# A causal mask for row maxima, moved from TensorE's identity matmuls to VectorE's fused add-and-max

## The reference

```python
qkv = jnp.einsum('bnd,ed->bne', inputs, w_in)
scores = jnp.einsum('bhqd,bhkd->bhqk', q, k) * Hd ** (-0.5)
causal = jnp.triu(jnp.ones((N, N), dtype=bool), k=1)
scores = jnp.where(causal, -jnp.inf, scores)
attn = jax.nn.softmax(scores, axis=-1)
out = jnp.einsum('bhqk,bhkd->bhqd', attn, v)
...
x = x + ga * _L0_attn_ref(h, ...)
h = _layernorm(x, axis=-1) * (1 + cb) + sb
x = x + gb * _L0_ffn_ref(h, ...)      # r * (square(relu(xk @ W_k.T)) @ W_v.T), r = sigmoid(xr @ W_r.T)
```

## Time and profile before

| | |
|---|---|
| Time, median of 3 runs | 1754.11 us (1753.4 to 1755.41) |
| Span of the profiled execution | 1747.5 us |
| The profiled execution's own time | not recorded apart from its span; the median lies 6.6 us above the span |
| Busy, share of the span | PE 84%, PEld 44%, DVE 67%, ACT 52%, POOL 42% |
| Instructions | PE 10024, DVE 2307, ACT 1795, POOL 876 |
| Mean granted TensorE clock | 0.930 |
| Chain that ended last, by engine | PE 49%, DVE 21%, issue 12%, ACT 9%, POOL 6% |

### The profile page before, as it was taken

How to read it: one execution, slowest core, us unless ns; L and a number is a source line. 1 busy time by engine, 2 the same in 40 slices (tenths; PEclk the granted TensorE clock), 3 DMA queues, 4 the chain that set the end, 5 groups by cost and what they waited for, 6 DMA issues and landing times.

```text
span 1747.5 us, 33032 instructions
## 1 busy us (share of the span) xinstructions
PE 1460.0 (84%) x10024; PEld 767.3 (44%) x10024; DVE 1176.4 (67%) x2307; ACT 911.6 (52%) x1795; POOL 731.7 (42%) x876
## 2 busy tenths in 40 slices
PE   2599999889897888879888898978889799889754
PEld 2343435444543445444444445434454344544344
DVE  4368677867677775767767775787757777677232
ACT  1146555555565554555555554555545655555622
POOL 2213213445344443544334553344434443444555
PEclk8679999899998999999998999989999999999966
DMA  3111113111311113111221113111131111211200
GB/s 103 38 64 57 45 57 100 44 50 55 99 56 35 56 57 97 57 42 51 74 79 41 54 56 95 58 39 54 53 94 66 39 51 65 67 56 44 60 28 18
DMA packets 101873, 102.98 MB, mean 59 GB/s; under 512 B 21296, under 2 KB 89912, under 8 KB 101696
## 3 DMA queue, kind: packets, MB, share of 16 engines
q1 hardware_dynamic: 99136, 92.38, 16.3%
q0 software_dynamic: 2560, 8.39, 1.3%
HBM read 31.74 MB, written 8.94 MB: 23 GB/s over the span
## 4 chain that ended last, share of the span: by engine, by line
PE 49%; DVE 21%; issue 12%; ACT 9%; POOL 6%; SPq 2%; DMA 1%; DVEq 1%; ACTq 0%; POOLq 0%
PE row_ps L1058 9%; PE val_ps L1082 9%; PE col_ps L1028 7%; PE dense_ps L1092 7%; DVE max_a L855 6%; PE dense_ps L1093 5%; PE dense_ps L1094 5%; ACT weights L699 4%; DVE mixed L968 2%; DVE max_b L855 2%; PE row_ps L1063 2%; PE dense_ps L1111 2%; SPq L457 2%; DVE xn_c L894 1%; DVE gated L952 1%
## 5 line engine op out<-in xcount | busy, mean ns | idle before, releaser
L699 ACT ACTIVATE weights<-col_ps 128x512 f32<-128x512 f32 (+1 forms) x1216 | 621.0, 580 | 475.3 <-PE col_ps L1028 473.4
L855 DVE TENSOR_REDUCE max_a<-row_ps 128x1 f32<-128x512 f32 (+3 forms) x864 | 550.1, 663 | 249.1 <-PE row_ps L1063 162.1
L1058 PE MATMUL row_ps<-k_stack,q_stack 96*128 96x512 bf16 (+3 forms) x1536 | 470.8, 345 | 52.6 <-DVE max_a L855 32.4
L1028 PE MATMUL col_ps<-q_stack,k_stack 99*128 99x512 bf16 (+3 forms) x1536 | 400.2, 337 | 52.2 <-ACT weights L699 32.3
L590 POOL TENSOR_SCALAR_AFFINE_SELECT weights<-weights 128x512 f32<-128x512 f32 x256 | 170.1, 664 | 557.9 <-ACT weights L699 555.9
L1082 PE MATMUL val_ps<-weights,v_ones 128*32 128x512 f32 (+3 forms) x3072 | 336.5, 511 | 15.5 <-POOL weights L590 15.2
L1058 PEld LDWEIGHTS row_ps<-k_stack,q_stack 96*128 96x128 bf16 x1536 | 147.4, 100 | 353.9 <-DVE max_a L855 166.8
L855 DVE TENSOR_REDUCE max_b<-row_ps 128x1 f32<-128x384 f32 (+3 forms) x352 | 213.2, 635 | 120.4 <-PE row_ps L1063 120.1
L1028 PEld LDWEIGHTS col_ps<-q_stack,k_stack 99*128 99x128 bf16 x1536 | 133.9, 99 | 219.8 <-ACT weights L699 136.8
L1063 PE MATMUL row_ps<-causal,ident_bf 128*128 128x128 bf16 x1024 | 208.5, 228 | 0.0
L1063 PEld LDWEIGHTS row_ps<-causal,ident_bf 128*128 128x128 bf16 x1024 | 104.9, 102 | 15.0 <-issue 0.7
(11 more groups left out here) (128 smaller groups left out, 2290.0 us busy)
## 6 DMA issues: line engine op xcount, KB each, us to landing
q_stack<-q_part SPq DMA_DIRECT2D x384, 64.0 KB, 2.6
k_stack<-k_part SPq DMA_DIRECT2D x384, 64.0 KB, 2.6
xa<-in_x SPq DMA_DIRECT2D x8, 1024.0 KB, 6.4
att<-val_out SPq DMA_DIRECT2D x64, 128.0 KB
recips<-recip_rows SPq DMA_DIRECT2D x32, 256.0 KB
xq<-in_x SPq DMA_DIRECT2D x28, 256.0 KB, 3.2
out<-xq POOLq DMA_DIRECT2D x28, 256.0 KB, 2.6
q_stack<-max_rows SPq DMA_DIRECT2D x192, 4.0 KB
```

The lines of the kernel that those rows point to most:

```text
L699: nc.scalar.activation(weights[:, t % 2, h:h + n, 0:q1 - q0], col_ps[bank][:, 0:n * (q1 - q0)].rearrange("p (h q) -> p h q", h=n), ACT.Exp ...
L855: nc.vector.reduce_max(dest, bank[:, 0:len(heads) * (k1 - k0)].rearrange("p (h k) -> p h k", h=len(heads)), AX_X).then_inc(max_done, 1)
L1028: last = nc.tensor.matmul(col_ps[bank][:, i * (q1 - q0):(i + 1) * (q1 - q0)], k_stack[s % 2][:, h, P * j:P * (j + 1)], q_stack[s % 2][:, h ...
L1058: last = nc.tensor.matmul(bank[:, n * width:(n + 1) * width], q_stack[stack][0:ROWS, h, P * i:P * (i + 1)], k_stack[stack][0:ROWS, h, k0:k ...
```

## The change

TensorE's masking matmuls are gone. `causal` becomes 512 wide, zeros and then the triangle in its last 128 columns. On VectorE each head of a diagonal unit gets one fused instruction that reads the scores from PSUM and the last `width` columns of `causal` from SBUF, adds them, writes the sum back over the scores in PSUM, and takes the maximum of the sum along the row. Plain units keep their maximum. The wait of every maximum is now one by `wait_apart`. To make room in SBUF, `recept` is dropped: ScalarE writes its tanh into `mix_out` itself, so it waits for `out_done` of the quarter before (VectorE waited for that until now).

```diff
-        causal = sb("causal", [P, P], BF16)
+        causal = sb("causal", [P, HALF], BF16)
...
-        recept = sb("recept", [P, 2, D])
...
                 if u == 10:
                     act.wait_ge(ready["recept"], q + 1)
-                    wait(act, free["value"], q)
-                    nc.scalar.activation(recept[:], dense_ps[:], ACT.Tanh, scale=0.5).then_inc(free["recept"], 1)
+                    wait(act, out_done, q)
+                    nc.scalar.activation(mix_out[:], dense_ps[:], ACT.Tanh, scale=0.5).then_inc(free["recept"], 1)
...
-                dve.wait_ge(rows_ready, at + 1)
+                wait_apart(dve, "dve", rows_ready, at + 1)
...
-                dest = (max_b[:, i - 4] if second else max_a[:, i])[:, heads[0]:heads[-1] + 1]
-                nc.vector.reduce_max(dest, bank[:, 0:len(heads) * (k1 - k0)].rearrange(
-                    "p (h k) -> p h k", h=len(heads)), AX_X).then_inc(max_done, 1)
+                dest, width = max_b[:, i - 4] if second else max_a[:, i], k1 - k0
+                if k1 == P * (i + 1):
+                    for n, h in enumerate(heads):
+                        scores = bank[:, n * width:(n + 1) * width]
+                        last = nc.vector.tensor_tensor_reduce(scores, scores, causal[:, HALF - width:], 1.0, MASKED,
+                                                              ALU.add, ALU.max, dest[:, h:h + 1])
+                    last.then_inc(max_done, 1)
+                else:
+                    nc.vector.reduce_max(dest[:, heads[0]:heads[-1] + 1],
+                                         bank[:, 0:len(heads) * width].rearrange("p (h k) -> p h k", h=len(heads)),
+                                         AX_X).then_inc(max_done, 1)
...
                 if u == 14:
                     dve.wait_ge(ready["value"], q + 1)
-                    wait(dve, out_done, q)
-                    nc.vector.scalar_tensor_tensor(mix_out[:], recept[:], 1.0, dense_ps[:], ALU.add, ALU.mult
+                    nc.vector.scalar_tensor_tensor(mix_out[:], mix_out[:], 1.0, dense_ps[:], ALU.add, ALU.mult
...
-                                            start=(n == 0), stop=(end and not diagonal), skip_group_check=True)
-                    if diagonal:
-                        last = nc.tensor.matmul(bank[:, (n + 1) * width - P:(n + 1) * width], ident_bf[:],
-                                                causal[:], start=False, stop=end, skip_group_check=True)
+                                            start=(n == 0), stop=(n == len(heads) - 1), skip_group_check=True)
```

More of the change, by code:

```diff
@@ L569, in _ @@
                                         pattern=[[-1, P]], channel_multiplier=1)
-            nc.gpsimd.affine_select(out=causal[:], in_=causal[:], compare_op=ALU.is_ge, fill=MASKED, base=0,
-                                    pattern=[[-1, P]], channel_multiplier=1).then_inc(consts_done, 1)
+            nc.gpsimd.affine_select(out=causal[:, HALF - P:], in_=causal[:, HALF - P:], compare_op=ALU.is_ge,
+                                    fill=MASKED, base=0, pattern=[[-1, P]], channel_multiplier=1
+                                    ).then_inc(consts_done, 1)
             pool.wait_ge(consts_done, 1)
@@ L1054, in row_unit @@
                 stack = (s + 1) % 2
-                diagonal = k1 == P * (i + 1)
                 for n, h in enumerate(heads):
-                    end = n == len(heads) - 1
                     last = nc.tensor.matmul(bank[:, n * width:(n + 1) * width],
```

## The result

The changed kernel takes 1822.05 us (1820.87 to 1827.36, 4 runs) against 1753.76: 1.040 times as long, interval 1.0376 to 1.0423, 68 us slower. The forecast was 16. The direction holds; the time lies outside the forecast's own range (1758 to 1800) and, by 3 us, inside the outer one, which ran to 1825. That outer part was put in for another rival, the held read, so that it held the result is luck.

A forecast was written before the change was run, and what follows sets the result against it. It took the kernel as coupled, TensorE with 49% of the chain and VectorE 21%. VectorE +44, TensorE -30 and tanh +2 gave +16 on 1747.5, with the median's 6.6 us 1770 us; own range 1758 to 1800, outer 1736 to 1825.

The forecast's parts named there:

- the held read: Rival on VectorE: the result's read waits until the fused instruction is through; +93 us, 1847 us, chance 0.12.
- how much of it lands on the end: Step taking 24% of VectorE's added 184 us as reaching the span's end: 44 us (26 low, 108 high).
- TensorE's saving: 1024 masking matmuls go from TensorE: 30 us gained, bounds 17 to 61.
- VectorE's prices: VectorE's added work: elements 18 us, reads 123, separate waits 43; 184 us in all (143 low, 348 high).
- The read: VectorE's read of each fused result: 0.12 us, bounds 0.08 to 0.28; 123 us for 1024 reads.
- The separate waits: VectorE's wait as its own instruction: 0.12 us more at 358 starts where it stands waiting, 43 us.
- The tanh: ScalarE's tanh into `mix_out` waits for the add, uncovered only in the drain: 2 us, bounds 0 to 8.
- The extra work hides: Rival: VectorE's added work falls into its idling for TensorE and the masks come off; about -25, 1729 us, chance 0.26.
- no change: Rival: the low ends of the terms meet; -2 us, 1752 us, chance 0.11.
- Half rate of the write back: Rival: VectorE's PSUM write takes turns with its read; 343 us more VectorE work, above 1900 us, chance 0.04.
- The clock: Rival: TensorE, with less work, sits at 1.2 GHz for 4% more of the span; +33 together, 1787 us, chance 0.04.
- What would show it: Signs: VectorE busy 1310 us, pair 0.72 before the next, TensorE's maxima waits above 203, VectorE's row waits below 363.

The follow-up runs named there:

- hold: GpSimd's last step of each group waits until VectorE has cut the second half's maxima; added to the kernel before: 1746.6 us, 0.9976.
- masks_off: The kernel before without TensorE's 1024 masking matmuls, row maxima taken over unmasked scores: 1720.7 us, 0.9857.
- before_late_hold: The kernel before with one short VectorE instruction ahead of the second cut of the maxima, and GpSimd's last step waiting for that cut: 1747.0 us, 1.0007.
- masks_off_fill: The kernel before without masking matmuls, plus 704 extra VectorE maxima over 40 columns, 75 us in all: 1755.6 us, 1.0025.
- after_hold_single: The changed kernel with GpSimd's last step waiting for the cut, fused instruction only in one-head units, others plain maxima over unmasked scores: 1761.7 us, 1.0063.
- before_late: The kernel before with one short VectorE instruction more ahead of the second cut of the maxima, 32 in all: 1790.1 us, 1.0258.
- after_hold: The changed kernel with GpSimd's last step of each group waiting until VectorE has cut the maxima: 1781.5 us, 1.0174.
- masks_off_hold: The kernel before without masking matmuls, maxima over unmasked scores, and GpSimd's last step waiting for VectorE's cut: 1739.1 us, 0.9935.

## Why the prediction was wrong

**The sum, as the runs divide it.** With the collision held off, the parts can be had one after the other: hold in the kernel before -4, masks off -7 (0.9976 to 0.9935), fused instructions with their waits on diagonal units +17 (to 1.0033), tanh into `mix_out` +7 (to 1.0075), separate waits on the other units +17 (to 1.0174), and the collision let in again +40 (to 1.040). Each step is uncertain by 5 to 11 us, so of the small ones -4 is not clear of nothing and -7 and +7 hardly are; 40 is. Together +70, and without the collision +30, which lies inside the forecast's 4 to 45 slower. The order matters: without the hold, masks_off gains 25 us, because it also pulls the cut clear of the select.

**The step that failed** is "how much of it lands on the end". It took what VectorE does more, 184 us, times a share of 24%. That step knows only two outcomes for added work, hidden or passed on. The trace of before held a third: a short instruction that waits behind GpSimd's, with the next, longer GpSimd instruction right after. There 0.2 us of lateness makes the cut 1 us longer in 15 groups more, and this overlap, which before_late_hold takes away, is worth 43 us. This term, 40 us of the 52 by which I was short, is not in the sum. The forecast named what was queued behind a late maximum (layer norm, `gated`, `mixed`), but not the cut, and it never set VectorE's short instructions beside GpSimd's timeline. The sign was there to read: in the earlier trace rows the steps of the cut of the first half take 0.17 us, while in the same trace the last step of the second half took 0.64.

**TensorE's saving,** -30: measured -25 by itself, 27 and 37 when matmuls were added, and 7 with the hold. The size was right for the kernel as it stood.

**VectorE's prices.** Elements 18 us: borne out (a fused instruction costs as much by width as a maximum). The read: taken 0.12, bounds 0.08 to 0.28, measured 0.05 to 0.06 where it is longest and 0.04 on average; 1024 of them are 38 to 61 us instead of 123. So VectorE got at most 73 us of elements and reads, not 141 (8 x (0.65 + 0.52 + 0.38 + 0.25) = 14.4 us a group against 12.1, 32 groups), and by the average 56. The error was in the fast direction and hid part of the other.

**The separate waits:** in the forecast 43 x 0.24 = 10; alone in the kernel before 12, with 4 more collided cuts in it. In the changed kernel with the hold those on plain units and transposes alone are worth 17, uncertain by 11.

**The share.** 17 us of 73, 23%, for the fused part (30% of 56; the waits ahead of it are in the 17); 39% for masks_off_fill, which has some collision in it; 41% for after_hold_single, which has none. These are uncertain by 9, 15 and 23 points. The 24% is at the low end, and the runs don't settle a better number.

**The tanh,** 2 (0 to 8): measured 9 and 7, each uncertain by 4 to 8. I looked for uncovered handovers in the drain alone. Where the rest arises I did not trace.

**The rivals.** *The extra work hides* and *no change* fall: the ratio's interval begins at 1.0376. *The read is held* falls by the timeline: it starts 0.65 us after the start of a fused instruction that lasts 0.73, and the next instruction starts with it. The time itself, 1822, lies where this rival's part of the range was; that is no support for it. The section "The DRAIN you can't avoid" of the Trainium skill's page "VectorE: DVE Perf Modes", which I quoted for it, goes on to say that a next instruction that is not held starts earlier, and the trace agrees with that. *Half rate of the write back* falls: 711 ns, not 1340. *The clock:* it did fall, 0.930 to 0.898 in the profiled executions, but less work on TensorE doesn't lower it (masks_off), and refilling TensorE doesn't help. Part of the fall goes with the collision: the executions of before_late have 0.908 to 0.928, those of before_late_hold 0.929 to 0.948. The collision isn't the only thing that lowers it: after_hold, without it, still has 0.911 to 0.918, and masks_off_hold 0.916 to 0.936.

So part of the 43 and 40 us probably reaches the end by way of the clock. In the profiled executions TensorE is busy for 36 us longer in before_late than in before_late_hold, and for 20 us longer in the changed kernel (1458.4) than in after_hold (1438.5), with the same instructions. Its waits for the cut are longer by 20 and 31 us. If half of the longer rows lands, as TensorE holds 49% of the chain, that makes 38 and 41 us. This is an estimate; no run holds the clock still, and how the loss divides stays open.

**What would show it.** Busy VectorE 1310 or more: 1269. The pair 0.72 before the next: 0.65. TensorE's waits for maxima rose from 203 to 267 us (138.2 + 67.5 + 61.7 in its weight loads) and VectorE's for rows fell from 363 to 348, as expected. Of the groups shown, s=1 kept its length, and s=2 and s=3 grew, where I had expected s=1 to grow and s=3 hardly.

Here are the two lists that hold these sums. Weight loads:

```profile
PEld row_ps L1065 <- DVE max_a L864: 138.2, 190, 2.5
...
PEld row_ps L1065 <- DVE max_a L860: 67.5, 114, 1.7
PEld row_ps L1065 <- DVE max_b L860: 61.7, 95, 1.7
```

VectorE:

```profile
DVE row_ps L860 <- PE row_ps L1065: 269.1, 244, 5.4
DVE max_a L864 <- PE row_ps L1065: 79.0, 97, 2.1
```

**A faster version.** No version with the fused instruction beats the kernel before; the nearest is 1.0033 with the hold, fewer separate waits and the buffer back. The kernel before with the hold stands at 0.9976, which may be nothing. Both faster ones, 0.9857 and 0.9935, leave out the mask of the row maxima.

## What to carry to other kernels

Before pricing a delay as "work times a share", lay the two engines' timelines over each other at the point where the delayed engine runs short instructions on SBUF beside GpSimd: if one of them already lasts as long as GpSimd's, the next one is a few tenths of a microsecond away from doing the same. When a time moves more than the added work can, look for instructions whose mean duration changed (here 397 to 614 ns and 194 to 378 ns on 16 columns) and then test by delaying the other engine on purpose. A gain or a loss measured by undoing one part is valid for the schedule around it: the same masks were worth 25 us or 7.

## What the hardware showed that I had not expected

- VectorE instructions of 16 columns take 0.17 us alone and 0.64 or 1.20 beside a GpSimd select or subtraction that started at the same time or just before, and end with it; both forms met this, the cast with one SBUF input and the subtraction with two.
- The read of the fused instruction's result lasts 0.14 us by its row, but where no wait stands behind it the next instruction starts at the same moment; a pair costs 0.04 us more than a maximum on average, up to 0.06.
- Reading a PSUM bank while writing back to it costs nothing that the 512-wide rows show beyond 711 against 683 ns.
- 6 us of VectorE work in all, placed badly, cost 43; one wait of GpSimd took all of it back.
